# A graph-attention kernel: each unit of 512 edges gathered once into a ring, and steps that pair units with node tiles through tables

## The reference, cut to what matters

```python
h = (x @ W).reshape(n, HEADS, OUT_C)
a1 = jnp.sum(h * attn_l, axis=-1); a2 = jnp.sum(h * attn_r, axis=-1)
e = jax.nn.leaky_relu(a1[src] + a2[dst], negative_slope=0.2)
ex = jnp.exp(e - seg_max[dst])
alpha = ex / jax.ops.segment_sum(ex, dst, num_segments=n)[dst]
out = jax.ops.segment_sum(h[src] * alpha[:, :, None], dst, num_segments=n)
```

## Time and profile before

| | us |
|---|---|
| median of 3 runs (2703.47 to 2704.06) | 2703.74 |
| the profiled execution, its own time | 2703.09 |
| its span, first to last instruction | 2701.3 |
| PE busy, share of the span | 2022.1, 75% |
| DVE busy | 1756.2, 65% |
| POOL busy | 1669.7, 62% |
| ACT busy | 876.5, 32% |
| bytes moved by DMA, mean rate | 347.19 MB, 129 GB/s |
| granted TensorE clock, mean | 0.856 |

### The profile page before, as it was taken

One profiled execution on the slowest core, in us unless ns is written; L12 is line 12 of the kernel. 1 busy time (PEld: TensorE's weight loads), 2 busy tenths in 40 slices (PEclk: granted clock), 3 DMA queues, 4 the chain that ended last, 5 costly groups with the idle time before them and its releaser, 6 DMA issues.

```text
span 2701.3 us, 30424 instructions
## 1 busy us (share of the span) xinstructions
PE 2022.1 (75%) x8324; PEld 1408.4 (52%) x8324; DVE 1756.2 (65%) x3687; ACT 876.5 (32%) x1728; POOL 1669.7 (62%) x1817
## 2 busy tenths in 40 slices
PE   7577677767766777677767766887788756799997
PEld 5344444444444544454445444665565543477776
DVE  6467666766666667666766666777777788333334
ACT  3433333333333333333333333222222233333332
POOL 4477777777777777777777777777777772000000
PEclk9788888888888888888888888787888877899999
DMA  8455555555555555555555555565555541100000
GB/s 264 143 144 142 144 144 146 141 145 144 146 141 145 144 145 142 144 144 144 142 145 144 146 139 150 158 165 159 163 161 163 152 133 46 32 18 17 17 17 25
DMA packets 174810, 347.19 MB, mean 129 GB/s; under 512 B 38366, under 2 KB 91204, under 8 KB 174660
## 3 DMA queue, kind: packets, MB, share of 16 engines
q0 software_dynamic: 83104, 233.87, 32.7%
q1 hardware_dynamic: 90468, 110.76, 13.7%
q10 hardware_dynamic: 1088, 0.79, 0.1%
HBM read 318.95 MB, written 26.33 MB: 128 GB/s over the span
## 4 chain that ended last, share of the span: by engine, by line
PE 28%; POOL 21%; issue 19%; DMA 14%; DVE 13%; ACT 4%; DVEq 1%; ACTq 0%; POOLq 0%; SPq 0%
POOL work L632 21%; DMA work<-h_tab,cols 13%; PE bank L1040 11%; PE bank L1100 6%; PE bank L1090 4%; DVE acc L1449 2%; DVE zs L1375 2%; PE bank L991 1%; ACT work L716 1%; PE bank L879 1%; ACT work L714 1%; DVE work L1441 1%; DVE zb L1376 1%; PE bank L932 1%; DVE zb L1378 1%
## 5 line engine op out<-in xcount | busy, mean ns | idle before, releaser
L632 POOL DMA_INDIRECT work<-h_tab,cols x1708 | 1617.9, 947 | 523.0 <-issue 451.4
L1040 PE MATMUL bank<-work 128*128 128x264 f32 x3416 | 1108.7, 472 | 528.0 <-DVE acc L1449 483.1
L1040 PEld LDWEIGHTS bank<-work 128*128 128x128 f32 x3416 | 743.5, 230 | 766.0 <-DVE acc L1449 562.4
L1441 DVE TENSOR_TENSOR work<-work,bank 128x1024 f32<-128x1024 f32 x427 | 519.1, 1216 | 111.0 <-issue 106.7
L722 ACT ACTIVATE bank<-zb 128x64 f32<-128x64 f32 x214 | 48.7, 228 | 1442.9 <-DVE zb L1380 1442.9
L1375 DVE TENSOR_REDUCE zs<-bank 128x128 f32<-128x384 f32 x214 | 119.2, 557 | 436.7 <-DMA work<-h_tab,cols 435.0
L1449 DVE TENSOR_TENSOR acc<-bank,acc 128x264 f32 x854 | 366.3, 429 | 50.6 <-DVE acc L1449 40.9
L1290 DVE TENSOR_TENSOR work<-bank,cols 128x1024 f32<-128x1024 f32 x215 | 261.0, 1214 | 0.0
L716 ACT ACTIVATE work<-work,ones 128x1024 bf16<-128x1024 bf16 x215 | 246.8, 1148 | 7.0
L714 ACT ACTIVATE work<-work,pcol 128x1024 bf16<-128x1024 bf16 x215 | 243.5, 1133 | 12.2 <-DMA work<-dst_d 12.2
L659 POOL COPY work<-acc 128x768 f32 (+2 forms) x17 | 13.6, 803 | 353.7 <-PE bank L1054 274.5
(11 more groups left out here) (255 smaller groups left out, 1818.3 us busy)
## 6 DMA issues: line engine op xcount, KB each, us to landing
work<-dst_d SPq DMA_DIRECT2D x216, 256.0 KB, 3.8
work<-h_tab,cols POOLq DMA_INDIRECT x1708
xnt_c<-xnt_d SPq DMA_DIRECT2D x66, 128.0 KB, 3.8
h_tab<-acc SPq DMA_DIRECT2D x49, 132.0 KB, 3.0
xnt_d<-acc SPq DMA_DIRECT2D x49, 128.0 KB, 3.2
q2t_d<-q2t_c SPq DMA_DIRECT2D x49, 128.0 KB, 1.9
out<-wqkv SPq DMA_DIRECT2D x16, 384.0 KB, 2.4
X<-x SPq DMA_DIRECT2D x5, 1024.0 KB, 10.5
```

Of the source, the lines that this page charges most:

```text
L632: nc.gpsimd.indirect_dma_start(out=ring[q][:, j, :], out_offset=None, in_=h_tab, in_offset=bass.IndirectOffsetOnAxis(ap=srcT[:, b * TB + j ...
L1040: ins = mm(bank[MB[(q * SB + s) % len(MB)]][:, 0:TW], hot[q][:, s * G + g, :], ring[q][:, s * G + g, :], start=(g == 0), stop=(g == G - 1))
L1441: v.tensor_tensor(m, m, ex, ALU.mult).then_inc(msg_ready, 1)
```

## The change

**Units.** G becomes 4: a unit has 512 edges, U = 403, STEPS = 451, and a batch has SB = 2 steps, again 8 blocks of 128 edges; NB = 226. POOL gathers each unit once, 403 * 4 = 1612 gathers, into a ring of RU = 5 units. A straddling unit is worked on in two steps from the same place of the ring. So the slot of a step is a number that is only known when the destinations have been counted: three tables in `t_tab` hold, per batch, the node tiles, the two ring slots and how many units must be there (`t_prog`, read by DVE), and per unit the step after whose scaling its slot is free (`t_free`, read by POOL). They are made in the first pass by `programs` and `frees`.

**POOL.** For each unit from the fifth on it loads one value of `t_free` into a register and waits for `msg_ready` of that step, where before it waited for `summed`, with a constant. Three gathers of a unit are issued, then POOL waits for the landing of all four of the unit before, tells it by `units_in`, and issues the fourth (ANNOUNCE = 3).

**DVE.** `program` loads four values per batch (two tiles, two slots), `exponents` one more and waits for `units_in`. `scale` reads the ring at the slot and writes one of MS = 3 buffers `M`; the denominators go there too, by ACT, one instruction per step. One step has twice the edges, so there are two `add` per batch instead of four; `one_hots` is made one batch ahead (HQ = 2 buffers). From batch FIN on two tiles per batch are divided and added, over 23 batches instead of 11, ACT sums all of them in the loop, and the square root for the first 44 is taken in the last batch; the row of PE that sums over nodes starts after it.

**First pass.** The sources come by two plain DMAs from SP, POOL fetches only the destinations (4 indirect DMAs instead of 14). **Experts.** The first expert's W1 comes in two halves, PE waits for each as it needs it, and all three W1 loads are on SP; b1 is loaded from ACT.

```diff
-G = 2
+G = 4
-SB = 4
-LAG = 2
+SB = 2
+LAG = 1
+RU = 5
+MS = 3
+HQ = 2
+ANNOUNCE = 3
-FT = 4
+FT = 2
...
-            def batch(i, q, side, first):
-                b = i * R3 + q
-                for j in range(len(steps_of(b)) * G):
...
-                    if j % G == 0:
-                        wait(pool, summed, SB * (b - R3) + j // G + 1)
-                        pool.sem_inc(step_begun, 1)
+            def announce(u):
+
+                pool.wait_ge(gathered[u % RU], 16 * G * (u // RU + 1))
+                pool.sem_inc(units_in, 1)
+
+            def unit(u):
+                if u >= RU:
+                    scaled = pool.value_load(t_free[0:1, u - RU:u - RU + 1], min_val=1, max_val=STEPS)
+                    pool.wait_ge(msg_ready, scaled)
+                    pool.sem_inc(unit_begun, 1)
+                r = u % RU
+                for g in range(G):
+                    if u and g == ANNOUNCE:
+                        announce(u - 1)
                     nc.gpsimd.indirect_dma_start(
-                        out=ring[q][:, j, :], out_offset=None, in_=h_tab,
-                        in_offset=bass.IndirectOffsetOnAxis(ap=srcT[:, b * TB + j:b * TB + j + 1], axis=0)).then_inc(gathered[q], 16)
+                        out=work[:, (r * G + g) * TW:(r * G + g + 1) * TW], out_offset=None, in_=h_tab,
+                        in_offset=bass.IndirectOffsetOnAxis(ap=srcT[:, u * G + g:u * G + g + 1], axis=0)).then_inc(gathered[r], 16)
...
-            def exponents(b, q, n):
+            def exponents(b, q, slots):

-                dve.wait_ge(gathered[q], n * 16 * TB - (SB - len(steps_of(b))) * 16 * G)
+                need = dve.value_load(t_prog[0:1, b * PR + PR - 1:b * PR + PR], min_val=1, max_val=U)
+                dve.wait_ge(units_in, need)
...
-                def scale(k):
+                def scale(s):

-                    m = ring[q][:, k * 4:k * 4 + 4, 0:C].rearrange("p j (h c) -> p j h c", h=H)
+                    m = M[(b * SB + s) % MS][:, :, 0:C].rearrange("p j (h c) -> p j h c", h=H)
+                    a = raw(slots[s])[:, :, 0:C].rearrange("p j (h c) -> p j h c", h=H)
...
                 scale(0)
-                if not begin:
-                    add(-2)
-                if not last:
-                    scale(1)
                 if not begin:
                     add(-1)
                 if last:
                     x2_var(0)
                 if not last:
-                    one_hots(b + 2, (q + 2) % R3)
+                    scale(1)
+                    one_hots(b + 1)
...
+                if last:
+                    x2_scale(0)
                 add(0)
-                add(1)
-                if a < e and not last:
+                if a < e:
                     plus(a, e)
```

More of the change, by code:

```diff
@@ L54 @@
 ROW = 448
-ROWS = [4, 5, 6, 7][-(KS // ROW):]
+SU = (U + 1) * G
+SD = NB * TB
+PR = 5
 NONE = 16384
@@ L223, in build @@
         ucol = view(KCH)
+        iotam = view(-(-KS // RU) * RU).bitcast(I32)
+        kmod = view(KS)
+        wmod = view(P)
+        wind = view(1)
+        ends = view(UCH)
+        turn_s = view(KS)
         tcol = view(KCH)
@@ new lines, in seg_gathers @@
+            def seg_gathers():
+                with pool.Fori(0, NB * SB) as k:
+                    row = pool.value_load(t_src[0:1, bass.ds(k, 1)], min_val=0, max_val=U * G)
+                    for g in range(G):
+                        j = k * G + g
+                        pool.wait_ge(seg_hot, j + 1)
+                        nc.gpsimd.tensor_copy(seg_i[:], srcT[:, bass.ds(row + g, 1)]).then_inc(seg_idx, 1)
+                        pool.wait_ge(seg_idx, j + 1)
+                        pool.sem_inc(seg_begun, 1)
+                        nc.gpsimd.indirect_dma_start(
+                            out=seg_rows, out_offset=None, in_=h_tab,
+                            in_offset=bass.IndirectOffsetOnAxis(ap=seg_i[:, 0:1], axis=0)).then_inc(seg_in, 16)
+                pool.wait_ge(seg_hot, NB * TB + 1)
@@ L636, in batch @@
+            for u in range(U):
+                if u == 1:
+                    pool.wait_ge(ext_ready, 1)
+                    nc.gpsimd.partition_all_reduce(amax[:, 1, :], amax[:, 0, :], P, RMAX).then_inc(ext_all, 1)
+                if u == RU:
                     pool.wait_ge(flag_ready, 1)
@@ L722, in weights @@
                 nc.scalar.activation(pk_ex, u, ACT.Exp).then_inc(ex_ready, 1)
-                nc.scalar.activation(ring[q][:, :, C:TW], u, ACT.Exp).then_inc(den_ready, 1)
+                for s in steps_of(b):
+                    n = b * SB + s
+                    wait(act, summed, n + 1 - MS)
+                    nc.scalar.activation(M[n % MS][:, :, C:TW], u[:, s * G:(s + 1) * G, :], ACT.Exp).then_inc(den_ready, 1)
             nc.scalar.copy(acc[:, A_COLS:], small[:, 31:32].to_broadcast([P, NT * TW - A_COLS])).then_inc(acc_zero, 1)
@@ L763, in batch @@
                     transposed(b + 2, (q + 2) % R3, i + 1 if q < 1 else i + 2)
-                if FIN < b < NB - 1:
-                    for t in range(XS * (b - FIN - 1), XS * (b - FIN)):
-                        sums(t)
+                for t in range(*finished(b - 1)):
+                    sums(t)
                 if side == "kv" and q == 1:
@@ L1366, in _, with program, raw @@
             dve.wait_ge(acc_zero, 2)
-            def exponents(b, q, n):
-                dve.wait_ge(gathered[q], n * 16 * TB - (SB - len(steps_of(b))) * 16 * G)
+            def program(b):
+                lo, hi = max(0, 1 - b), LAG + 1 if b == NB - 1 else PR - 1
+                _, r = nc.values_load_multi_w_load_instructions(
+                    t_prog[0:1, (b + 1) * PR + lo:(b + 1) * PR + hi], engines=[mybir.EngineType.DVE], min_val=0,
+                    max_val=(NT - 1) * TW, skip_runtime_bounds_check_because="steps' node tiles and ring slots are bounded")
+                r = (None,) * lo + tuple(r)
+                return r[0:SB], [nc.s_assert_within(n, 0, (RU - 1) * RW, skip_runtime_bounds_check_because="a slot of the ring")
+                                 for n in r[SB:2 * SB]]
+            def raw(slot):
+                return work[:, bass.ds(slot, RW)].rearrange("p (j w) -> p j w", w=TW)
+            def exponents(b, q, slots):
+                need = dve.value_load(t_prog[0:1, b * PR + PR - 1:b * PR + PR], min_val=1, max_val=U)
+                dve.wait_ge(units_in, need)
                 dve.wait_ge(a2c_picked, b + 1)
```

323 lines of the change are left out of this document (173 added, 150 removed).

## The result

| | us |
|---|---|
| the changed kernel, median of 4 runs (2601.92 to 2610.59) | 2606.76 |
| the kernel before beside it, median of 4 | 2703.9 |
| ratio, with its 95% interval | 0.9636 (0.9624 to 0.9647) |
| the profiled execution of the change, its own time | 2610.59 |
| its span | 2608.8 |

97 us faster, 3.6%, where the prediction had 135. The direction was right, and so was where the gain comes from (fewer gathers by POOL at the same pace); 38 us of the gain (42 in the profiled execution) did not come.

What follows compares the result with a forecast made beforehand. The prediction took POOL's gathers, one per 1.25 us, as the bound. 2703.1 - 120.1 (fewer gathers) + 8 (landing waits) - 12.6 (from FIN on) - 9.4 (after the loop) = 2569.0 us; range 2553 to 2610.

Steps and rivals of the forecast that it cites:

- Fewer gathers: POOL's loop: 1612 gathers instead of 1708 at an unchanged 1.2512 us each, 120.1 us off.
- The slot's register load: POOL, per unit from the fifth on: loading the scaling step to wait for costs nothing; bounds nothing to 0.66 us per unit.
- Waiting for landings: POOL before each unit's fourth gather: landings over 4.2 us delay it, 8 us more, between 0 and 35.
- the flag's load: POOL between its 24th and 25th gather before the change: a register load that left them 1.25 us apart, so taken as hidden.
- rival 3: POOL after each unit's last gather: the slot's register load stands open, up to 0.66 us 398 times, +263, 2832 us; chance 0.05.
- The consumers: PE and DVE at 8.93 us per batch: they keep up, PE needing 8.0 in the mix stage; cost 0, at most 10 us.
- From FIN on: Last batches of the loop: DVE takes 9.1 us each, last scaling 12.7 us after last gather instead of 25.3, 12.6 us off.
- After the loop: Last scaling to PE's sum over the nodes: some 3.7 us instead of 13.1, 9.4 us off.
- First pass: Before the gathers: index gathers go, table work on DVE comes; taken as 0, between -7 and +6 us.
- the backlog: From FIN on: DVE's 9.1 us per batch against POOL's 8.93 leaves DVE 4 us behind over 22 batches.
- Landings ruling POOL: Mix stage: each fourth gather waits for a landing at 4.8 us, 53 us instead of 8, 2614 us; chance 0.07.
- Rival 4: Loop: gathers are not the bound, a batch keeps 10.01 us and 12 more batches cost 120, 2801 us; chance 0.02.

Runs made afterwards that it cites:

- the repeat: The changed kernel unedited, run again on another chip: 2601.4 us, ratio 0.9621 to the kernel before.
- both_ends: Changed kernel with landing wait two gathers later, sources loaded with the 23rd first-pass tile, weights' sums moved from 21st to 29th tile: 2568.1 us.
- sources_late: Changed kernel with SP's two source loads issued with the 23rd first-pass tile instead of ahead of the first: 2602.5 us, the change beside it 2601.4.
- the first four runs: Four edits of the changed kernel (landing wait moved three ways; register load doubled): 3323.2, 3319.8, 3303.6 and 3343.0 us, kernel before 3113.0 beside them.

## Why the prediction was right or wrong, point by point

- **Fewer gathers, -120.1: right.** 1612, a median of 1.254 apart in this profile and 1.251 in the repeat. The 2.5 ns between them are 4 us of the profiled execution's 41.6 over the forecast; the repeat does not have them.
- **The slot's register load, 0: right.** Doubling it costs 0.07 us per load, nearly all of it behind late landings. The Trainium skill's floor of some 600 ns for such a load ("DMA: Bandwidth & Descriptors", Latency and other measured facts) would have made it 239 us. In POOL's list the trace is not far from it (0.29 us for the load, 0.15 for its address arithmetic, 0.56 from the start of the load to the wait behind it); as a cost in the sum the floor does not hold.
- **Waiting for landings, 8 between 0 and 35: mechanism and limit right, size wrong.** It is 22.5 (20.8 in the repeat). The limit of 4.2 us was right: of the 370 units whose landings are all recorded, 56 landed later than 4.2, by 22.0 us in sum, and 56 fourth gathers have more than 0.35 us of idle, by 22.0 beyond the common 0.30. Two steps failed. The first: the prediction's own rows gave 10.7 for the mix stage and 5 for the qk stage, 15.7 in sum, and it then took 8 without a reason. The second is the count in the qk stage. I took the last landings of batches from the chain of waits, where in the qk stage five of 147 passed 4.2, as if they stood for all. In the change POOL waits for every unit, also those in the middle of what was a batch, about which the chain said nothing. By stage the fourth gathers have 12.2 us above the grid in the qk stage (13.0 in the repeat) where the rows gave 5, and 9.7 in the mix stage (7.3) where they gave 10.7. The landings are 2.7 us at least, 3.0 in the median and 5.5 at most. The Trainium skill's fit of 2.0 us and the bytes at 436 GB/s ("DMA: Bandwidth & Descriptors", Anatomy of one DMA), which would have made this term nothing, is below all of them; where the two differ the measurement decides. The Trainium skill also has the latency of memory grow with its load ("DMA: Bandwidth & Descriptors", Latency and other measured facts), and the spread is in keeping with that; no run here varied the load alone.
- **What POOL's lead was worth: not in the sum.** This step failed in kind and not only in size, some 14 us. I priced the wait itself and not what had been hidden by the lead that it takes. I used the lead as an argument (the flag's load, rival 3) and asked only whether the new load fits in. The pauses every 100 gathers were never to be seen in the trace of before, where gathers are 1.25 apart throughout, and could not have been priced from it; that something unseen would come out could have had a bound. Moving the wait by two gathers took 32 us off the loop at once, and the kernel then came to 2572, 3 us from the forecast. Part of that nearness is luck: in the profiled execution of that kernel (2577.5) the loop is 4 us shorter than the forecast's, and the first pass and what follows the last gather are 12 longer.
- **The consumers, 0: right.** The 38 waits for scalings are of the common 0.3. PE's need in the mix stage was put at 8.0 of 8.93; it is 7.2 (394.05 us busy in 500 of the repeat, times the 9.1 us of its batch), at a granted clock of 0.87 there instead of 0.81.
- **From FIN on, -12.6: right.** Batches 8.88 apart (predicted 9.1), the last scaling 12.8 us after the last gather (12.7).
- **After the loop, -9.4: 2.5 too much.** PE's sum starts 6.2 us after the last scaling, not 3.7. I had 0.5 for the reciprocal; DVE waits 2.25 for the root, which ACT gives after its last sums and a table load of 1.28 us. The Trainium skill has 1283 ns for such a load ("ScalarE activation tables: per-element evaluation and per-set limits", What a function is on this engine), and the trace agrees; I had not looked which functions ACT changes between there.
- **First pass, 0 between -7 and +6: wrong by 6.5**, just outside its bounds in this profile, by 3 in the repeat. The table work was known and costed; that it falls on the same tile as the sums of the weights was to be read in the lists and was not. The two apart (both_ends) took 2 us off PE's wait. The loads on SP ahead of the first store, which I had also blamed, are worth nothing (sources_late), and the rest of the 6.5 is not put down to anything.
- **The range.** Its own low end, 2553, does not come out of what it names: 2569 less 8, 7 and the 4 of the backlog is 2550. Nothing hangs on it. The measured time lies near the upper end because several terms missed on the same side.
- **The rivals.** Landings ruling POOL (2614) came nearest in time, but at 4.8 us each in one stage, which is not what is seen. Rival 4, that gathers are not the bound and 12 batches more cost, had 2%; something of its kind may be what the chip of the first four runs shows, where the variants were 6 to 7% slower than before. That the bound can be another one on another chip was in no case of mine.

41.6 us over the forecast in the profiled execution, in round parts: 14.5 landings, some 15 second gathers, 3.5 the median interval (1.2537 instead of 1.2512), 6.5 the first pass, 2.5 the end.

## What to carry to other kernels

Where a queue runs ahead of the engine that it feeds, that lead is a resource. A wait put into it costs not only when it is late but lays open what the lead hid, and things show up that the old trace cannot show. So put the wait as late as the consumer allows (here two gathers later, with the same signal for DVE, 29 us), and when pricing one, ask how far ahead the queue was. Where rows give a term, take what they give, and ask which cases they leave out. And where one engine sets the pace, adding busy time to another can cost nothing at all (here 435 us), so shares of busy time say little.

## What was not expected of the hardware

- A doubling of PE's sums raised the mean granted clock from 0.856 to 0.979, and the kernel before took 2703.8 us instead of 2703.6.
- In the change POOL's indirect gathers pause by up to 1.6 us beyond the common 0.3 at 12 of 16 places that lie 100 gathers apart, and still at the same places with three more instructions per unit. With the wait two gathers later six of them are left, and the kernel before, whose POOL waits for no landing, shows none.
- On one chip the kernel before took 3113 us instead of 2704, and four variants of the change 3304 to 3343, with the same durations of gathers and only the loop slower. Two of these edits are 3% and 5% faster than the kernel before on other chips and 7% slower there.
